# Attention with experts on one core: the row maxima turned by two column-tiled products and sent in one transfer, router logits and experts' sum placed earlier

## The chip, the cores and the metric

One Trainium2 chip, one of its cores. The metric is the device time of one launch in microseconds (us).

## The reference

32 sequences of 256 tokens, 128 wide, pass one pre-norm layer: attention with 16 heads of 8 dimensions, whose softmax is replaced by a rational "stablemax", then a mixture of four experts of which the two with the highest router logits are used.

```python
def stablemax3(logits):                      # over the keys
    logits = logits - max(logits)            # the row maximum
    s = where(x >= 0, 1 + x*(1 + x/2*(1 + x/3)), 1/(1 - x*(1 - x/2*(1 - x/3))))
    return s / sum(s)

x = x + (stablemax3(q @ k.T * hd**-0.5) @ v) @ w_out.T + b_out   # q, k, v of layernorm(x)
xf = layernorm(x)
gates = top-2 of softmax(xf @ router_w + router_b), made to sum to 1
h = silu(einsum('td,edf->etf', xf, w1)) * einsum('td,edf->etf', xf, w3)
x = x + einsum('te,etd->td', gates, einsum('etf,efd->etd', h, w2))
```

## The kernel before, in words

Each sequence ("batch" n, 0 to 31) is one unit of work. A hand-written software pipeline runs over them: `over_batches` calls `first_half` and `second_half` of every engine for n = -2 to 3 written out, for 4 to 27 in a loop of two batches a turn, and for 28 to 31 written out; then `drain`. The engines are TensorE (PE), VectorE (DVE), ScalarE (ACT), GpSimd (POOL) and SyncE (SP, which only issues transfers). Each has its own fixed list of instructions, and semaphores alone join them. From n = 2 on the code takes the branch `settled(n)`.

In the first half of n the core forms the distances of every score from its row's maximum. PE multiplies `q_pad` by `k_stack` (`distances`, L1363), and two rows of `q_pad`, 124 and 125, hold the maxima as a high and a low part, against ones in `k_stack`; so the subtraction is part of the product. ACT squares them (L640), DVE makes a polynomial (L886). Between these PE does the up products of batch n-2's experts: `up_a_unit` and `up_b_unit`, six products each (L1277), whose `a` side goes through silu on ACT (L649) and is multiplied with the `b` side on DVE (`hidden`, L878). POOL weights the hidden units with the gates (L465), which come through DRAM (`gate_scratch`, `gate_all`).

In the second half of n the core forms the scores of batch n+1 (`scores`, L1533), of which DVE keeps only each row's maximum (`scores_max`, L971, eight instructions into `mx`). ACT turns the polynomials of batch n into weights (logarithm L744, exponential L749), PE multiplies them with the values (`weighted_values`, L1295, four groups; products of 32 columns in four column tiles) and forms the experts' down products of batch n-2 (`down`, L1550).

The stretch that the change touches is the end of the second half and the start of the next first half. On PE it is, in this order: weighted values 0 and 1; `maxima_T` (L1594), two transposes that turn `mx` (tokens by heads) into `misc` (16 rows by 256 tokens); `up_a_unit` 0; `queries_and_keys` of batch n+2 (L1277 into `misc`, so it waits for `m_ok`, when the maxima have been read out of it); `router_logits` of batch n-1 (L1584; it waits for `acc_ok`, since the experts' sum lies in the same bank); weighted values 2; `up_b_unit` 0 (waits for `lg_ok`); and then, in the first half, distances 0 and 1 (they wait for the transfers into `q_pad`, `m_stacked`), the values product (L1388, waits for `qk_out`), weighted values 3, the up units 1, distance 2 (waits for polynomial 0).

On DVE it is: the last maximum; `maxima_out`, which adds 1 and splits the maxima into a high part rounded to fp32r (L1020) and the rest (L1022); `experts_added` (L996, signals `acc_ok`); the copy of queries and keys (L985, signals `qk_out`); the logits with their bias (L1003), their maximum and shift (L1010, L1013), four comparisons (L1029, L1030, signal `compared`); four gate steps (L1039, L1042, L1045, L1049), of which the first waits for POOL's `rank` and for ACT's `exp_l` (L793); the input statistics (L858); then hidden 0 and polynomials 0 and 1 of the first half. ACT comes from the last exponential of weights (L749) to `exp_l`, loads a table (L632), does silu 0 and squares 0 and 1. POOL ranks the logits (L567 to L579), adds a bias (L589) and splits queries and keys (L481, L484). SP sends the maxima's two parts, one transfer each (L418, L421), then the output (L426), the gates (L431), and in the first half the queries and keys.

Of the kernel before, what the change touches and what calls it, by code (L numbers as in the profile page):

```python
# [5 lines left out]
def attention_then_experts_kernel(nc: bass.Bass, x: bass.AP, w_qkv: bass.AP, w_out: bass.AP, b_out: bass.AP,  # L6
# [20 lines left out]
    F32 = mybir.dt.float32  # L27
    F32R = mybir.dt.float32r
# [30 lines left out]
    with ctx:  # L59
# [33 lines left out]
        mx = sb("mx", [128, C, H])  # L93
        m_split = sb("m_split", [H, 2, S], F32R)
# [237 lines left out]
        def _(sp):  # L332
# [73 lines left out]
            def second_half(i, off):  # L406
# [8 lines left out]
                if has(i, off + 1):  # L415
                    par = (off + 1) % 2
                    sp.wait_ge(mx_hi_ok, m_split_at)
                    sp.dma_start(q_pad[par][MROW:MROW + 1, :, :, :].bitcast(F32),  # L418
                                 m_split[:, 0, :].bitcast(F32)).then_inc(m_stacked[par], 16)
                    sp.wait_ge(m_ok, m_split_at)  # L420
                    sp.dma_start(q_pad[par][MROW + 1:MROW + 2, :, :, :].bitcast(F32),  # L421
                                 m_split[:, 1, :].bitcast(F32)).then_inc(m_stacked[par], 16)
# [417 lines left out]
        def _(dve):  # L840
# [97 lines left out]
            def second_half(i, off):  # L938
# [29 lines left out]
                def scores_max(u):  # L968
                    dve.wait_ge(s_full, U * (n + 1) + u + 1)
                    by_row = mx[:].rearrange("p c (g j) -> p j c g", j=2)  # L970
# [45 lines left out]
                def maxima_out():  # L1016
                    m = n + 1
                    dve.wait_ge(mT_full, m + 1)
                    after(dve, m_stacked[off % 2], pair_count(i, off, 32))
                    nc.vector.tensor_scalar(m_split[:, 0, :], misc[0:H, 0:S], 1.0, None, ALU.add).then_inc(mx_hi_ok, 1)  # L1020
                    dve.wait_ge(mx_hi_ok, m + 1)
                    nc.vector.scalar_tensor_tensor(m_split[:, 1, :], misc[0:H, 0:S], 1.0, m_split[:, 0, :].bitcast(F32),  # L1022
                                                   ALU.add, ALU.subtract).then_inc(m_ok, 1)
# [29 lines left out]
                if settled(n):  # L1053
# [13 lines left out]
                    if has(i, off + 1):  # L1067
                        scores_max(U - 1)
                        maxima_out()
                    experts_added()  # L1070
                    if has(i, off + 2):
                        queries_and_keys_copied()
                    biased_logits()
                    shifted_logits()
                    compare()
                    for k in range(GATE):
                        gate_step(k)
                    if has(i, off + 3):
                        input_statistics(n + 3)
# [180 lines left out]
        def _(pe):  # L1260
# [86 lines left out]
            def distances(i, off, u):  # L1347

                m, par = no(i, off), off % 2
                if u == 0:  # L1350
                    pe.wait_ge(s_used, U * (m + 1))
                    pe.wait_ge(stacked[par], pair_count(i, off, STACKED))
                    pe.wait_ge(m_stacked[par], pair_count(i, off, 32))
# [13 lines left out]
            def first_half(i, off):  # L1367
# [64 lines left out]
                if settled(n):  # L1432
                    distance(0)
                    distance(1)
                    values()
# [75 lines left out]
            def second_half(i, off):  # L1511
# [75 lines left out]
                def maxima_T():  # L1587
# [5 lines left out]
                    for c in range(C):  # L1593
# [210 lines left out]
```

## Time and profile before

| | us |
|---|---|
| three runs | 1168.31 to 1169.56, median 1169.13 |
| the profiled execution | 1168.15, its span 1166.4 |
| PE busy | 1117.6 (96%) |
| DVE busy | 989.8 (85%) |
| ACT busy | 1002.8 (86%) |
| POOL busy | 746.7 (64%) |

The granted TensorE clock of the profiled execution is 0.995. The span is that of the traced instructions; the execution's own time adds 1.75 us around it. Busy shares are means over the whole span. A batch takes about 34.5 us and its stretches look alike from batch to batch, so one batch in the middle is read instruction by instruction. PEld is PE's loading of weights, which overlaps its products; a product's end in the trace is modelled, so for PE the distances between starts are read.

### The profile page before, as it was taken

How to read it: one execution, taken by the hardware profiler on the slowest of the kernel's cores; microseconds unless marked ns; L12 is line 12 of the kernel's file. 1: busy time of each engine (PE TensorE's matmuls, PEld its weight loads, DVE VectorE, ACT ScalarE, POOL GpSimd, SP SyncE). 2: the span in 40 equal slices, each digit the busy share in tenths (PEclk: the TensorE clock that was granted, in tenths of full speed). 3: DMA queues.
4: the chain of work that ended last, by engine and by line, in shares of the span. 5: the costliest groups of instructions: out<-in, count | busy, mean ns of one | idle time of the engine just before them, and what ended most of it. 6: DMA issues, size and time to landing. Idle time of an engine off the chain costs nothing.

```text
span 1166.4 us, 29175 instructions
## 1 busy us (share of the span) xinstructions
PE 1117.6 (96%) x9904; PEld 942.5 (81%) x9904; DVE 989.8 (85%) x1789; ACT 1002.8 (86%) x1034; POOL 746.7 (64%) x999
## 2 busy tenths in 40 slices
PE   6889999999999999999999999999999999999998
PEld 5758888888888788887888888888887888888888
DVE  4889888899888889888889988888988888988844
ACT  0799899988889998888998888989888899888982
POOL 5347666767666677666676766676766667766530
PEclk8999999999999999999999999999999999999999
DMA  4443333233332233333223333223333222333100
GB/s 127 163 138 115 115 98 92 79 123 115 120 104 89 85 100 117 118 112 94 87 85 118 118 123 100 85 80 113 117 118 107 93 84 94 118 120 108 41 6 11
DMA packets 130063, 117.49 MB, mean 101 GB/s; under 512 B 16452, under 2 KB 124644, under 8 KB 130020
## 3 DMA queue, kind: packets, MB, share of 16 engines
q1 hardware_dynamic: 127812, 113.78, 31.8%
q10 hardware_dynamic: 2208, 3.15, 0.9%
q8 instruction: 26, 0.43, 0.1%
q14 instruction: 17, 0.14, 0.0%
HBM read 94.70 MB, written 21.09 MB: 99 GB/s over the span
## 4 chain that ended last, share of the span: by engine, by line
PE 57%; DVE 14%; issue 12%; POOL 8%; ACT 4%; DMA 2%; DVEq 1%; SPq 0%; ACTq 0%; POOLq 0%
PE banks L1277 23%; PE banks L1550 12%; PE sc L1363 8%; DVE mx L971 5%; DVE poly L886 3%; PE banks L1295 3%; POOL hid L465 3%; PE sc L1533 3%; ACT w_sq L640 1%; PE misc L1277 1%; DMA gate_all<-gate_scratch 1%; ACT poly L744 1%; PE misc L1410 1%; PE misc L1428 1%; PE sc L1277 1%
## 5 line engine op out<-in xcount | busy, mean ns | idle before, releaser
L465 POOL TENSOR_TENSOR hid<-hid,gate_all 128x512 f32<-128x512 f32 x240 | 376.9, 1635 | 155.0 <-DMA gate_all<-gate_scratch 155.0
L886 DVE SCALAR_TENSOR_TENSOR poly<-w_sq,sc 128x1024 f32<-128x1024 f32 x252 | 303.5, 1215 | 23.9 <-ACT w_sq L640 23.6
L1277 PE MATMUL banks<-xn_hi,w_hi 128*128 128x256 f32 x976 | 295.2, 302 | 10.3 <-DVE hid L878 9.7
L640 ACT ACTIVATE w_sq<-sc 128x1024 f32<-128x1024 f32 x252 | 255.3, 1028 | 36.6 <-PE sc L1363 35.6
L1277 PE MATMUL banks<-xn_lo,w_hi 128*128 128x256 f32 x976 | 275.0, 282 | 0.0
L1277 PE MATMUL banks<-xn_hi,w_lo 128*128 128x256 f32 x976 | 274.3, 281 | 0.0
L744 ACT ACTIVATE poly<-poly,two 128x2048 f32<-128x2048 f32 x128 | 252.1, 1992 | 0.4
L1550 PE MATMUL banks<-w_sb,hid 128*128 128x128 f32 x1920 | 247.6, 282 | 0.7 <-POOL hid L465 0.7
L971 DVE TENSOR_REDUCE mx<-sc 128x4 f32<-128x1024 f32 x192 | 230.6, 1216 | 11.0 <-PE sc L1533 9.2
L1550 PEld LDWEIGHTS banks<-w_sb,hid 128*128 128x128 f32 x1920 | 224.1, 191 | 17.7 <-POOL hid L465 1.6
L749 ACT ACTIVATE poly<-poly 128x2048 f32<-128x2048 f32 x128 | 236.7, 1895 | 0.0
L1277 PEld LDWEIGHTS banks<-xn_hi,w_hi 128*128 128x128 f32 x976 | 183.2, 188 | 60.3 <-issue 25.2
L649 ACT ACTIVATE silu_a<-banks 128x512 f32<-128x512 f32 x240 | 144.1, 600 | 59.2 <-PE banks L1277 42.9
L1277 PEld LDWEIGHTS banks<-xn_lo,w_hi 128*128 128x128 f32 x976 | 183.7, 188 | 3.9
L1277 PEld LDWEIGHTS banks<-xn_hi,w_lo 128*128 128x128 f32 x976 | 183.8, 188 | 0.0
L1363 PE MATMUL sc<-q_pad,k_stack 128*128 128x512 f32 x504 | 158.9, 406 | 6.6 <-DVE poly L886 5.3
L878 DVE TENSOR_TENSOR hid<-silu_a,banks 128x512 f32<-128x512 f32 x240 | 160.6, 679 | 0.4
L1295 PE MATMUL banks<-poly,v_pad 128*32 128x256 f32 x2048 | 130.6, 384 | 1.0 <-DVE mx L971 0.7
L1363 PEld LDWEIGHTS sc<-q_pad,k_stack 128*128 128x128 f32 x504 | 78.6, 188 | 18.5 <-DVE poly L886 13.0
L1295 PEld LDWEIGHTS banks<-poly,v_pad 128*32 128x32 f32 x2048 | 56.8, 109 | 40.0 <-issue 7.2
L567 POOL TENSOR_TENSOR equal<-equal,earlier 128x16 f32<-128x16 f32 x62 | 12.3, 220 | 119.7 <-DVE equal L1030 119.7
L971 DVE TENSOR_REDUCE mx<-banks 128x4 f32<-128x1024 f32 x64 | 77.9, 1217 | 0.4 <-PE sc L1533 0.4
(186 smaller groups left out, 1441.4 us busy)
## 6 DMA issues: line engine op xcount, KB each, us to landing
qk_scratch<-qk_split SPq DMA_DIRECT2D x32, 512.0 KB, 3.1
k_tile<-qk_scratch SPq DMA_DIRECT2D x128, 128.0 KB, 2.6
q_pad<-qk_scratch SPq DMA_DIRECT2D x256, 64.0 KB
q_tile<-qk_scratch SPq DMA_DIRECT2D x124, 128.0 KB, 2.5
k_stack<-qk_scratch SPq DMA_DIRECT2D x124, 128.0 KB
gate_all<-gate_scratch SPq DMA_DIRECT2D x30, 512.0 KB, 4.5
x_in<-in_L_attn_x_dram SPq DMA_DIRECT2D x32, 128.0 KB, 2.1
x_res<-in_L_attn_x_dram SPq DMA_DIRECT2D x32, 128.0 KB, 2.3
```

Source lines behind the costliest of these rows:

```text
L465: nc.gpsimd.tensor_tensor(h, h, by_token.unsqueeze(1).to_broadcast([128, 2, C, 128]), ALU.mult).then_inc(gated, 1)
L640: nc.scalar.activation(w_sq[:, u % 2, :], distance_buf(n, u), ACT.Square).then_inc(sq_ok, 1)
L649: nc.scalar.activation(silu_a[:, u % 2, :], up_a[:], ACT.Silu).then_inc(silu_ok, 1)
L744: nc.scalar.activation(poly[:, C * g:C * (g + 1), :], poly[:, C * g:C * (g + 1), :], ACT.Ln, bias=two[:]).then_inc(ln_ok, 1)
L749: nc.scalar.activation(poly[:, C * g:C * (g + 1), :], poly[:, C * g:C * (g + 1), :], ACT.Exp, scale=-1.0).then_inc(p_ok, 1)
L878: nc.vector.tensor_tensor(hid[:, 2 * u:2 * u + 2, :].rearrange("p a t -> p (a t)"), silu_a[:, u % 2, :], b_bank[u], ALU.mult).then_inc(hid ...
L886: nc.vector.scalar_tensor_tensor(poly[:, u, :], w_sq[:, u % 2, :], 3.0, distance_buf(n, u), ALU.add, ALU.mult).then_inc(poly_ok, 1)
L971: nc.vector.tensor_reduce(by_row[:, :, :, u], score_buf[u].rearrange("p (j c t) -> p j c t", j=2, c=C), AX.X, ALU.min, negate=True).then_i ...
L1277: last = nc.tensor.matmul(dst, lhs[a], rhs[b], start=(k == 0), stop=(k == len(terms) - 1))
L1295: last = nc.tensor.matmul(pv[32 * j:32 * j + 32, g // 2, :], v_pad[par][:, c, 4 * g + j, first:first + 32], poly[:, 2 * g + j // 2, at:at ...
L1363: last = nc.tensor.matmul(dst[:, 2 * c * S:2 * (c + 1) * S], k_stack[par][:, u, c * 128:(c + 1) * 128], q_pad[par][:, u, :, :].rearrange(" ...
L1550: last = nc.tensor.matmul(up_b[:, c * D:(c + 1) * D], hid[:, FB * e + f, c * 128:(c + 1) * 128], w2_sb[:, FB * e + f, :], start=(e == 0 an ...
```

## The change

The layout of `mx` becomes heads by column halves, so that one row of it is 32 values, (head, half). `maxima_T` becomes two ordinary float32 products of `mx` (as weights, 32 columns) with the identity, one into rows 0 to 31 and the same again into rows 32 to 63 of `misc`, each 128 wide. `maxima_out` adds 1 and rounds all 64 rows in one instruction, and then overwrites rows 32 to 63 of `m_split` with the rest that rounding left. One transfer takes the 64 rows to both rows of `q_pad`; the waits on `m_stacked` count 16 and no longer 32 per batch. In the settled branch DVE adds the experts' sum ahead of `maxima_out`, takes the logits, their shift and the comparisons ahead of the copy of queries and keys, and the input statistics ahead of the gate steps. PE takes the router products right behind `maxima_T`, and the values product ahead of distances 0 and 1.

```diff
--- before.py
+++ after.py
@@ -90,8 +90,8 @@
         q_pad = [sb(f"q_pad{i}", [128, GP, 2, S], F32R) for i in range(2)]
         ones = sb("ones", [2, S])
         v_pad = [sb(f"v_pad{i}", [128, C, H, 48]) for i in range(2)]
-        mx = sb("mx", [128, C, H])
-        m_split = sb("m_split", [H, 2, S], F32R)
+        mx = sb("mx", [128, H, C])
+        m_split = sb("m_split", [64, 128], F32R)
         w_sq = sb("w_sq", [128, 2, 4 * S])
         poly = sb("poly", [128, U, 4 * S])
         o_T = sb("o_T", [128, G // 2, S])
@@ -414,12 +414,9 @@
                     sp.dma_start(x_in[:], batch_at(x, x_from)).then_inc(x_loaded, 16)
                 if has(i, off + 1):
                     par = (off + 1) % 2
-                    sp.wait_ge(mx_hi_ok, m_split_at)
-                    sp.dma_start(q_pad[par][MROW:MROW + 1, :, :, :].bitcast(F32),
-                                 m_split[:, 0, :].bitcast(F32)).then_inc(m_stacked[par], 16)
                     sp.wait_ge(m_ok, m_split_at)
-                    sp.dma_start(q_pad[par][MROW + 1:MROW + 2, :, :, :].bitcast(F32),
-                                 m_split[:, 1, :].bitcast(F32)).then_inc(m_stacked[par], 16)
+                    sp.dma_start(q_pad[par][MROW:MROW + 2, :, :, :].bitcast(F32),
+                                 m_split[:].bitcast(F32)).then_inc(m_stacked[par], 16)
                 if has(i, off - 2):
                     par = off % 2
                     sp.wait_ge(acc_ok, added)
@@ -967,7 +964,7 @@
 
                 def scores_max(u):
                     dve.wait_ge(s_full, U * (n + 1) + u + 1)
-                    by_row = mx[:].rearrange("p c (g j) -> p j c g", j=2)
+                    by_row = mx[:].rearrange("p (g j) c -> p j c g", j=2)
                     nc.vector.tensor_reduce(by_row[:, :, :, u], score_buf[u].rearrange("p (j c t) -> p j c t", j=2, c=C),
                                             AX.X, ALU.min, negate=True).then_inc(s_used, 1)
 
@@ -1016,11 +1013,11 @@
                 def maxima_out():
                     m = n + 1
                     dve.wait_ge(mT_full, m + 1)
-                    after(dve, m_stacked[off % 2], pair_count(i, off, 32))
-                    nc.vector.tensor_scalar(m_split[:, 0, :], misc[0:H, 0:S], 1.0, None, ALU.add).then_inc(mx_hi_ok, 1)
+                    after(dve, m_stacked[off % 2], pair_count(i, off, 16))
+                    nc.vector.tensor_scalar(m_split[:], misc[0:64, 0:128], 1.0, None, ALU.add).then_inc(mx_hi_ok, 1)
                     dve.wait_ge(mx_hi_ok, m + 1)
-                    nc.vector.scalar_tensor_tensor(m_split[:, 1, :], misc[0:H, 0:S], 1.0, m_split[:, 0, :].bitcast(F32),
-                                                   ALU.add, ALU.subtract).then_inc(m_ok, 1)
+                    nc.vector.scalar_tensor_tensor(m_split[32:64, :], misc[32:64, 0:128], 1.0,
+                                                   m_split[32:64, :].bitcast(F32), ALU.add, ALU.subtract).then_inc(m_ok, 1)
 
                 def compare():
                     for c in range(C):
@@ -1066,17 +1063,18 @@
                         queries_T()
                     if has(i, off + 1):
                         scores_max(U - 1)
+                    experts_added()
+                    if has(i, off + 1):
                         maxima_out()
-                    experts_added()
-                    if has(i, off + 2):
-                        queries_and_keys_copied()
                     biased_logits()
                     shifted_logits()
                     compare()
+                    if has(i, off + 2):
+                        queries_and_keys_copied()
+                    if has(i, off + 3):
+                        input_statistics(n + 3)
                     for k in range(GATE):
                         gate_step(k)
-                    if has(i, off + 3):
-                        input_statistics(n + 3)
                     return
                 statistics()
                 if isinstance(i, int) and n == -2:
@@ -1350,7 +1348,7 @@
                 if u == 0:
                     pe.wait_ge(s_used, U * (m + 1))
                     pe.wait_ge(stacked[par], pair_count(i, off, STACKED))
-                    pe.wait_ge(m_stacked[par], pair_count(i, off, 32))
+                    pe.wait_ge(m_stacked[par], pair_count(i, off, 16))
                     if isinstance(i, int) and 0 <= m < 2:
                         pe.wait_ge(ones_in[par], 16)
                 elif isinstance(i, int) and m < 2:
@@ -1430,9 +1428,9 @@
                     last.then_inc(res_full, 1)
 
                 if settled(n):
+                    values()
                     distance(0)
                     distance(1)
-                    values()
                     weighted_values(i, off - 1, 3)
                     ups(1)
                     distance(2)
@@ -1590,8 +1588,9 @@
                         pe.wait_ge(xn2_out, n)
                     if settled(n) and has(i, off + 2):
                         pe.wait_ge(xnT_ok, n + 3)
-                    for c in range(C):
-                        last = nc.tensor.transpose(misc[0:H, c * 128:(c + 1) * 128], mx[:, c, :], ident[:])
+                    for part in range(2):
+                        last = nc.tensor.matmul(misc[32 * part:32 * (part + 1), 0:128],
+                                                   mx[:].rearrange("p h c -> p (h c)"), ident[:], start=True, stop=True)
                     last.then_inc(mT_full, 1)
 
                 def queries_and_keys():
@@ -1635,10 +1634,10 @@
                     weighted_values(i, off, 1)
                     if has(i, off + 1):
                         maxima_T()
+                    router_logits()
                     up_a_unit(i, off - 1, 0)
                     if has(i, off + 2):
                         queries_and_keys()
-                    router_logits()
                     if isinstance(i, int) and n == B - 1:
                         up_b_unit(i, off - 1, 0)
                         late_up_a(LATE, 1)
```

PE, end of the second half of a settled batch, before (`xn2_hi` and `xn2_lo` are the experts' input, `w1` and `w3` the up weights, `rw` the router's; the last row of each piece opens the first half of the next batch, and rows that repeat are left out):

```order
L1594 MATMUL misc<-ident,mx 16x128 x2
L1277 MATMUL banks<-xn2_hi,w1_hi 128x256
...
L1277 MATMUL misc<-xn_split,proj_hi 128x256 x2
L1277 MATMUL misc<-xn_split,proj_lo 128x256
...
L1584 MATMUL banks<-rw,xn2_T 128x4 x2
L1295 MATMUL banks<-poly,v_pad1 32x256 x8
L1277 MATMUL banks<-xn2_hi,w3_hi 128x256
...
L1363 MATMUL sc<-q_pad0,k_stack0 128x512 x4
L1388 MATMUL misc<-proj_T,xn_T 128x128 x2
```

and now:

```order
L1592 MATMUL misc<-ident,mx 32x128 x2
L1582 MATMUL banks<-rw,xn2_T 128x4 x2
L1275 MATMUL banks<-xn2_hi,w1_hi 128x256
...
L1275 MATMUL misc<-xn_split,proj_hi 128x256 x2
L1275 MATMUL misc<-xn_split,proj_lo 128x256
...
L1293 MATMUL banks<-poly,v_pad1 32x256 x8
L1275 MATMUL banks<-xn2_hi,w3_hi 128x256
...
L1386 MATMUL misc<-proj_T,xn_T 128x128 x2
L1361 MATMUL sc<-q_pad0,k_stack0 128x512 x4
```

The router products have moved ahead of the up unit and of queries and keys, the values product ahead of the distances; the rest stands as it stood.

DVE, from the last maximum of a settled batch to the first hidden product of the next half, before:

```order
L1020 TENSOR_SCALAR m_split<-misc 16x256
L1022 SCALAR_TENSOR_TENSOR m_split<-misc,m_split 16x256
L996 TENSOR_TENSOR y_acc0<-banks,y_acc0 128x256
L985 COPY qk<-misc 128x512
L1003 TENSOR_TENSOR logits<-banks,router_b_all 128x4 x2
L1010 TENSOR_REDUCE top_l<-logits 128x2
L1013 TENSOR_TENSOR shifted<-logits,top_l 128x8
L1029 TENSOR_TENSOR above<-logits 128x16
L1030 TENSOR_TENSOR equal<-logits 128x16
...
L1039 SCALAR_TENSOR_TENSOR chosen<-rank,exp_l 128x8
...
L858 BN_STATS stats<-x_in 128x6 x2
L878 TENSOR_TENSOR hid<-silu_a,banks 128x512
```

and now:

```order
L993 TENSOR_TENSOR y_acc0<-banks,y_acc0 128x256
L1017 TENSOR_SCALAR m_split<-misc 64x128
L1019 SCALAR_TENSOR_TENSOR m_split<-misc,m_split 32x128
L1000 TENSOR_TENSOR logits<-banks,router_b_all 128x4 x2
L1007 TENSOR_REDUCE top_l<-logits 128x2
L1010 TENSOR_TENSOR shifted<-logits,top_l 128x8
L1026 TENSOR_TENSOR above<-logits 128x16
L1027 TENSOR_TENSOR equal<-logits 128x16
...
L982 COPY qk<-misc 128x512
L855 BN_STATS stats<-x_in 128x6 x2
L1036 SCALAR_TENSOR_TENSOR chosen<-rank,exp_l 128x8
...
L875 TENSOR_TENSOR hid<-silu_a,banks 128x512
```

The experts' sum has moved ahead of the split, the copy of queries and keys behind the comparisons, the statistics ahead of the gates.

## Rows read from the trace of the kernel before

**Rows 1.** The page's chain that ended last, by engine.

```profile
PE 57%; DVE 14%; issue 12%; POOL 8%; ACT 4%; DMA 2%; DVEq 1%; SPq 0%; ACTq 0%; POOLq 0%
```

**Rows 2.** Busy time by stretches: stretch, its length, busy time (and instructions) of each engine.

```profile
569.82:579.16 9.34, 8.53 (x81) 6.46 (x77) 6.45 (x21) 8.69 (x10) 4.34 (x10) 1.00 0.07 18
579.16:604.31 25.15, 25.14 (x227) 21.93 (x227) 24.11 (x35) 22.39 (x23) 19.27 (x22) 1.00 0.43 136
```

**Rows 3.** PE in time: start, us, what, records, idle before it and releaser.

```profile
569.82 0.39 PE L1594 MATMUL misc<-ident,mx 128*16 128x128 f32 x2
569.96 0.36 PE L1277 MATMUL banks<-xn_hi,w_hi 128*128 128x256 f32 x1
...
571.20 0.47 PE L1277 MATMUL misc<-xn_split,proj_hi 128*128 128x256 f32 x2 [0.29 <-issue]
...
571.99 0.50 PE L1584 MATMUL banks<-rw,xn_T 128*128 128x4 f32 x4
572.42 1.07 PE L1295 MATMUL banks<-poly,v_pad 128*32 128x256 f32 x16
573.42 0.39 PE L1277 MATMUL banks<-xn_hi,w_hi 128*128 128x256 f32 x1
...
574.24 1.07 PE L1363 MATMUL sc<-q_pad,k_stack 128*128 128x512 f32 x4
...
575.68 1.07 PE L1295 MATMUL banks<-poly,v_pad 128*32 128x256 f32 x16
...
578.03 0.39 PE L1277 MATMUL banks<-xn_hi,w_hi 128*128 128x256 f32 x1 [0.36 <-DVE hid L878]
...
579.16 0.73 PE L1363 MATMUL sc<-q_pad,k_stack 128*128 128x512 f32 x2 [0.15 <-DVE poly L886]
```

**Rows 4.** PE's weight load behind weighted values 2, in time.

```profile
573.42 0.19 PEld L1277 LDWEIGHTS banks<-xn_hi,w_hi 128*128 128x128 f32 x1 [0.41 <-issue]
```

**Rows 5.** DVE in time.

```profile
568.40 1.22 DVE L971 TENSOR_REDUCE mx<-sc 128x4 f32<-128x1024 f32 x1
570.24 0.41 DVE L1020 TENSOR_SCALAR m_split<-misc 16x256 fp32r<-16x256 f32 x1 [0.62 <-PE misc L1594]
570.69 0.41 DVE L1022 SCALAR_TENSOR_TENSOR m_split<-misc,m_split 16x256 fp32r<-16x256 f32 x1
571.03 0.40 DVE L996 TENSOR_TENSOR y_acc<-banks,y_acc 128x256 f32<-128x256 f32 x1
572.19 0.69 DVE L985 COPY qk<-misc 128x512 f32<-128x512 f32 x1 [0.76 <-PE misc L1277]
572.80 0.22 DVE L1003 TENSOR_TENSOR logits<-banks,router_b_all 128x4 f32<-128x4 f32 x2
...
575.17 0.41 DVE L1039 SCALAR_TENSOR_TENSOR chosen<-rank,exp_l 128x8 f32<-128x8 f32 x1 [1.41 <-POOL rank L579]
...
576.10 0.89 DVE L1049 TENSOR_TENSOR gates<-chosen,chosen_r 128x8 f32<-128x8 f32 x1
...
577.89 2.34 DVE L886 SCALAR_TENSOR_TENSOR poly<-w_sq,sc 128x1024 f32<-128x1024 f32 x2
```

**Rows 6.** ACT in time.

```profile
569.64 3.70 ACT L749 ACTIVATE poly<-poly 128x2048 f32<-128x2048 f32 x2
573.45 0.21 ACT L793 ACTIVATE exp_l<-shifted 128x8 f32<-128x8 f32 x1
...
575.61 1.94 ACT L640 ACTIVATE w_sq<-sc 128x1024 f32<-128x1024 f32 x2
```

**Rows 7.** POOL in time: its first split of queries and keys.

```profile
575.93 1.03 POOL L481 TENSOR_TENSOR qk_split<-qk,zero 128x512 fp32r<-128x512 f32 x1
```

**Rows 8.** Transfers by line: issues, KB each, median us from issue to landing.

```profile
q_pad<-m_split SPq DMA_DIRECT2D x64, 16.0 KB, 2.2
gate_scratch<-gates SPq DMA_DIRECT2D x30, 4.0 KB, 1.4
```

**Rows 9.** The page's DMA queues: packets, MB, share of 16 engines' span.

```profile
q1 hardware_dynamic: 127812, 113.78, 31.8%
```

## The prediction

> **What bounds the kernel now.** I read the page's chain first: PE carries 57% of the chain that ended last, DVE 14%, and 12% is "issue" [rows 1]. The kernel is a pipeline of nearly equal periods. I cut one of them in two with the view of busy time by stretches [rows 2]; its parts are 9.34 and 25.15 us long. From the maxima's turn (569.82) to the third distance product of the next batch (579.16) PE is busy 8.53 us; from there to the next turn (604.31) it is busy 25.14 us. The second piece is PE's alone and the change hardly touches it. Everything that can be won lies in the first 9.34 us, and every edit lies there.
>
> What PE waits for in this stretch is read from its starts in order of time [rows 3]. I price each block by the distance to the next start where nothing is waited for:
> - the turn, 569.82 to 569.96: 0.14
> - a unit of six up products, 573.42 to 574.24: 0.82; there are four of them in the stretch: 3.28
> - queries and keys, 571.20 to 571.99: 0.79
> - router products, 571.99 to 572.42: 0.43
> - a group of weighted values, 572.42 to 573.42: 1.00; two: 2.00
> - distances 0 and 1 with the values product, 574.24 to 575.68: 1.44
>
> Together 8.08 us. (The other group of weighted values, at 575.68, and the other up units have the same form.) The stretch takes 9.34, so PE stands still for 1.26 us in it: before the queries and keys (they wait for the maxima's split on DVE, m_ok, which ends at 571.10), before the second up_b unit (578.03; it waits for DVE's first hidden product) and before distance 2 (it waits for DVE's first polynomial, 577.89 and 1.22 long, so done at 579.11; PE goes on at 579.16) [rows 3, 5].
>
> Why is DVE late there? Before that polynomial it waits 0.62 for the turned maxima, 0.76 for the queries and keys and 1.41 for POOL's rank [rows 5]. The rank needs DVE's comparisons, the last of which ends at 573.76 (575.17 less 1.41), and these are late because the logits come last on PE and behind the copy of queries and keys on DVE.
>
> **The change, part by part.** I place everything on the clock of the period shown, with the last maximum ending at 569.62.
>
> Experts' sum ahead of the split: the 0.40 us of the sum [rows 5] now run from about 569.54 to 569.94, inside DVE's 0.62 us wait. Cost nothing; if the turn came at once instead, it would cost the split 0.3.
>
> The turn: two transposes of 16 columns become two float32 products of 32 columns, in two column groups. A float32 product is two records on this PE (four for the two router products at 571.99) [rows 3], so four records in place of two. Then the router follows at once, and it needs the experts' sum (acc_ok, at about 570.0). Its start is not in the trace. Lower bound: the sum's end and PE's reaction, 570.06, which is 0.10 later than the 569.96 at which PE now goes on. Upper bound: after a group of column-tiled products the full-width weight load stood still for 0.41 us [rows 4]; 0.41 on top of the old slot. I take 0.24, since the products are short (128 columns against 256 in the row with 0.41) and run in two groups at once. So PE's work is 8.08 + 0.24 = 8.32 us, between 8.18 and 8.49.
>
> The same weight-load gap bears on a rule: the Trainium skill, TensorEngine Tiling (Array Packing), section Tiling Modes, says that changing the tiling mode drains the engine, and under Restrictions that column tiling excludes the transpose mode for float32. By that rule the full-mode transposes now pay a drain after the weighted values, and tiled products would not pay it: only the drain behind them would remain, the change would add about nothing to PE, and the time would come out 28.5 x 0.24, some 7 us, under the sum below. The trace cannot tell this, since before the old turn the weight load waits 0.41 us for DVE's maximum as well.
>
> The split: each of its two DVE instructions walks 128 elements and not 256. The 128x512 copy takes 0.69 and the 16x256 instruction 0.41 [rows 5], so 256 elements are 0.28 and 128 are 0.14: 0.27 each. They end near 570.95 and not 571.10. PE reaches the queries and keys at 570.20 + 0.43 + 0.82 = 571.45, later than that: the first wait is gone, 0.45 us.
>
> Logits earlier: router products end near 570.75, DVE takes the logits at 570.95 right behind the split. From the logits to the last comparison's end there were 0.96 us (572.80 to 573.76), so now 571.9, where it was 573.76. POOL's rank between them and chosen took 1.41 us (573.76 to 575.17) [rows 5], so chosen could start at 573.3.
>
> What is late next is ACT: its last exponential of weights ends at 573.34 and exp_l came at 573.45 [rows 6]; it can come at 573.27, since the engines begin an instruction some 0.08 before the recorded end of the last one. Gain only 0.18 there. So chosen at about 573.55 and the gates done by 575.4, where they were 576.99 [rows 5]. Square 0 then starts 2.16 after exp_l, as it did (573.45 to 575.61, table load and silu 0 between them) [rows 6], at 575.43, ending 0.97 on (two take 1.94); polynomial 0 runs from 576.5 to 577.7. By ACT and DVE distance 2 could start at 577.75.
>
> Copy of queries and keys behind the comparisons: PE starts them at 571.45, the copy came 0.99 after their start (571.20 to 572.19) [rows 3, 5], so 572.45 to 573.15; DVE is free from 571.9, nothing is lost. Waiting for it: POOL's split of them (at 575.93 before [rows 7]) and now PE's values product. Input statistics ahead of the gates: 0.4 us of DVE, in the time that it would wait for exp_l.
>
> Values ahead of distance 0 on PE: PE comes there at 571.45 + 0.79 + 1.00 + 0.82 = 574.1, 0.9 us after the copy. No wait. Distance 0 moves to about 574.6, still before ACT needs it (575.43).
>
> One transfer for two on SP: issue at about 571.1, landing 2.2 us after [rows 8], 573.3; distance 0 wants it at 574.6. One issue less on SP, which has no one behind it.
>
> **Sum.** PE reaches distance 2 after 8.32 us, at 578.14; ACT and DVE would allow 7.93. PE decides. Gain per batch 9.34 - 8.32 = 1.02 us, with 0.85 and 1.16 at the bounds. From then on PE is the chain, and ACT and DVE follow it. The reordered part runs in 29 batches (2 to 30; the last has no queries and keys and gets half), so 28.5 x 1.02 = 29 us, and under 1 us in the filling. Against the profiled execution's 1168.15 that is 1139; the median of the runs shown is 1169.13, 1 us more, so I say **1139**.
>
> **Rivals.**
> (a) The turn costs PE nothing more: a gap ahead of the old transposes, hidden in the wait for the maximum, goes, and only one behind the products comes. Then PE's 8.08 decide, 9.34 - 8.08 = 1.26 per batch, 1132; ACT's 7.93 would allow 1.41 and 1128 at most. For it: the gap comes after every group of column-tiled products, wherever that stands. Against: the router still needs the experts' sum. Chance 0.10. This is the way the rule of the Trainium skill named above would have it.
> (b) DVE stays late. The gates instruction took 0.89 us for eight elements at 576.10 [rows 5], while POOL's split ran until 576.96 [rows 7]; POOL's split of queries and keys can now start earlier and hold it, twice if it falls badly, for about 1.3 us more. Then the gates are done at 576.6 and not 575.4, the polynomial starts 0.6 later as it did (hidden 0 lies between), lasts 1.22, and distance 2 comes at about 578.5 to 578.9: gain 0.4 to 0.8, 1145 to 1157, in the middle 1151. Chance 0.13.
> (c) The gain is given back in the second piece (by the gates' transfer, or by ACT), or PE's idle time only moves: within 0.2% of before, which is about what a measurement of this kernel can tell from no change. Against: 25.14 of 25.15 us there are PE's own work. Chance 0.05.
> (d) Slower, by the transfer. Two transfers of 16 pieces become one of 64 pieces into two partitions. Packets took 0.318 x 16 x 1166 / 127812 = 46 ns of one DMA engine each [rows 9]. If all 64 go through one engine, that is 3.0 us on top of 2.2: landing at 576.3, and distance 0 waits 1.7 us for it. It costs more than it gains once the landing takes 4.5 us: +0.7 per batch, 1188. Against: the gates' store, also of many small rows, lands in 1.4 us [rows 8]. Chance 0.07.
>
> **How the numbers follow.** The forecast has 0.65, (a) 0.10, (b) 0.13, (c) 0.05, (d) 0.07. Faster by over 0.2%: 0.88; within: 0.05; slower: 0.07. The forecast's own range is 1135 to 1144 from the bounds of the turn (28.5 x 1.16 and 28.5 x 0.85), and 2 us more on each side for starts read to a few hundredths; with most of (a) and (b) the range is 1130 to 1155, and (c), (d) stay outside.
>
> **What would show it.** In the changed profile: the period falls to about 33.5 us; PE's wait before the queries and keys is gone, and so are those for the first hidden product and for polynomial 0; the last comparison ends some 2.1 us after the turn's start and not 3.94; chosen waits for ACT's exp_l and not for POOL; the transfer lands in 2.1 to 2.5 us. It is wrong if distance 0 waits for a DMA, if the values product waits for DVE, or if the router's first record starts over 0.6 us after the turn.

## The result, and the profile after

The changed kernel takes 1129.05 us, median of 4 runs (1128.44 to 1130.74), against 1168.84 us before, median of 4 (1168.31 to 1169.56). The ratio is 0.966, 95% interval 0.9645 to 0.9678: 3.4% faster, about 40 us. The forecast was 1139 in a range from 1130 to 1155; the sign is right, the gain is a third larger than forecast, and the time lies 1 us below the range. The profiled execution took 1130.74 us with a span of 1129.0, so against the one of before (1168.15, span 1166.4) there are 37.4 us to explain.

The page's chain of the changed kernel, by engine, to be held against [rows 1]:

```profile
PE 90%; ACT 4%; DVE 3%; DMA 1%; issue 1%; ACTq 0%; SPq 0%; DVEq 0%
```

PE has gone from 57% to 90% of the chain. Busy time by stretches in the same columns as [rows 2], cut at the same places, the turn at 553.18 and the third distance product at 561.42:

```profile
553.18:561.42 8.24, 8.24 (x82) 6.25 (x79) 6.27 (x21) 8.21 (x11) 4.48 (x10) 1.00 0.16 51
561.42:586.42 25.00, 24.99 (x229) 21.91 (x227) 23.90 (x36) 22.98 (x25) 19.23 (x22) 1.00 0.41 126
```

The first piece has shrunk from 9.34 to 8.24 us and PE is busy in all of it. The second went from 25.15 to 25.00. The granted clock is 1.00 in both columns before and after, so none of this is the clock.

PE in time, which answers to [rows 3]:

```profile
553.18 0.39 PE L1592 MATMUL misc<-ident,mx 128*32 128x128 f32 x4
553.58 0.58 PE L1582 MATMUL banks<-rw,xn_T 128*128 128x4 f32 x4
554.01 0.37 PE L1275 MATMUL banks<-xn_hi,w_hi 128*128 128x256 f32 x1
...
554.81 0.40 PE L1275 MATMUL misc<-xn_split,proj_hi 128*128 128x256 f32 x2
...
555.61 1.07 PE L1293 MATMUL banks<-poly,v_pad 128*32 128x256 f32 x16
556.61 0.38 PE L1275 MATMUL banks<-xn_hi,w_hi 128*128 128x256 f32 x1
...
557.42 0.61 PE L1386 MATMUL misc<-proj_T,xn_T 128*128 128x128 f32 x4
557.79 1.17 PE L1361 MATMUL sc<-q_pad,k_stack 128*128 128x512 f32 x4
...
558.89 1.07 PE L1293 MATMUL banks<-poly,v_pad 128*32 128x256 f32 x16
559.89 0.39 PE L1275 MATMUL banks<-xn_hi,w_hi 128*128 128x256 f32 x1
...
561.42 0.62 PE L1361 MATMUL sc<-q_pad,k_stack 128*128 128x512 f32 x2
```

No row of PE's products carries a wait any more. The turn takes 0.40 us until the router products start (four records for two products, as read), and the queries and keys follow the up unit after 0.80 us without a gap. Two of PE's weight loads do stand still:

```profile
553.15 0.15 PEld L1592 LDWEIGHTS misc<-ident,mx 128*32 128x32 f32 x4 [0.27 <-DVE mx L968]
553.54 0.52 PEld L1582 LDWEIGHTS banks<-rw,xn_T 128*128 128x128 f32 x4 [0.24 <-issue]
```

The second is put down to no one, but it begins 0.12 us after the recorded end of the experts' sum (553.01 and 0.41 long, below), which the router products wait for by the program. The section on the order alone comes back to it.

DVE in time, which answers to [rows 5]:

```profile
551.88 1.22 DVE L968 TENSOR_REDUCE mx<-sc 128x4 f32<-128x1024 f32 x1
553.01 0.41 DVE L993 TENSOR_TENSOR y_acc<-banks,y_acc 128x256 f32<-128x256 f32 x1
553.62 0.28 DVE L1017 TENSOR_SCALAR m_split<-misc 64x128 fp32r<-64x128 f32 x1 [0.19 <-PE misc L1592]
553.94 0.28 DVE L1019 SCALAR_TENSOR_TENSOR m_split<-misc,m_split 32x128 fp32r<-32x128 f32 x1
554.25 0.23 DVE L1000 TENSOR_TENSOR logits<-banks,router_b_all 128x4 f32<-128x4 f32 x2
...
555.06 0.17 DVE L1027 TENSOR_TENSOR equal<-logits 128x16 f32<-128x16 f32 x1
555.72 0.69 DVE L982 COPY qk<-misc 128x512 f32<-128x512 f32 x1 [0.49 <-PE misc L1275]
556.33 0.47 DVE L855 BATCH_NORM_STATS2 stats<-x_in 128x6 f32<-128x128 f32 x2
557.02 0.45 DVE L1036 SCALAR_TENSOR_TENSOR chosen<-rank,exp_l 128x8 f32<-128x8 f32 x1 [0.22 <-ACT exp_l L790]
...
557.99 0.48 DVE L1046 TENSOR_TENSOR gates<-chosen,chosen_r 128x8 f32<-128x8 f32 x1
558.92 0.69 DVE L875 TENSOR_TENSOR hid<-silu_a,banks 128x512 f32<-128x512 f32 x1 [0.45 <-ACT silu_a L646]
559.89 2.35 DVE L883 SCALAR_TENSOR_TENSOR poly<-w_sq,sc 128x1024 f32<-128x1024 f32 x2 [0.29 <-ACT w_sq L637]
```

The reader is to see three things. The sum at 553.01 lies beside the turn, and of DVE's wait for the turned maxima 0.19 us are left, where there were 0.62. The last comparison ends at 555.23, 2.05 us after the turn's start (forecast 2.1, before 3.94). Chosen, hidden 0 and polynomial 0 now all wait for ACT: polynomial 0 is done at 561.11 and PE comes to distance 2 only at 561.42, so DVE is 0.3 us early and PE decides.

To see what one batch in the middle does not show, I took the starts of every PE block in the 27 periods from the first settled turn on, and their means, before and after (us from block start to the next block's start; worked out from the two traces):

```
                                         before   changed
turn, to the next block                   0.141     0.407
router products                           0.432     0.438
up_a 0 (before: with the wait for m_ok)   1.288     0.799
queries and keys                          0.786     0.801
weighted values 2                         1.001     1.000
up_b 0                                    0.817     0.815
distances 0, 1 and values                 1.443     1.463
weighted values 3                         1.001     1.001
up units 1 (before: with the wait)        2.472     1.533
= first piece                             9.38      8.26
distance 2                                0.569     0.463
two up units behind distance 3            1.521     1.443
second down block                         2.933     2.883
weighted values 0, 1, to the turn         1.867     1.774
= second piece, all blocks               25.21     24.96
period                                   34.59     33.22
```

A batch has gained 1.12 us in the first piece and 0.25 us in the second: 1.37 us, and 28 of them are 38 us. (The span shrank by 37.4: in this execution the first settled turn came 0.9 us later than before, 121.28 and not 120.41, and the end was 0.3 us shorter.)

### The profile page after: what moved, and what is told of

It is laid out like the page before. It is cut to its first block, busy times and chain, and to the rows that moved or that the text cites. A ratio compares the mean times of both kernels' runs of the same rounds, so it can differ in the third digit from the quotient of the medians.

```text
span 1129.0 us, 29283 instructions
## 1 busy us (share of the span) xinstructions
PE 1104.0 (98%) x9968; PEld 936.7 (83%) x9968; DVE 980.8 (87%) x1789; ACT 1004.1 (89%) x1034; POOL 750.7 (66%) x999
## 4 chain that ended last, share of the span: by engine, by line
PE 90%; ACT 4%; DVE 3%; DMA 1%; issue 1%; ACTq 0%; SPq 0%; DVEq 0%
PE banks L1275 33%; PE banks L1548 20%; PE sc L1361 11%; PE banks L1293 10%; PE sc L1531 4%; PE misc L1275 2%; ACT poly L741 2%; PE banks L1582 2%; ACT poly L746 1%; PE misc L1408 1%; PE misc L1426 1%; PE misc L1386 1%; PE banks L1531 1%; PE sc L1275 1%; DVE mx L968 1%
## 5 line engine op out<-in xcount | busy, mean ns | idle before, releaser
L1275 PE MATMUL banks<-xn_hi,w_hi 128*128 128x256 f32 x976 | 289.3, 296 | 0.2
L1361 PE MATMUL sc<-q_pad,k_stack 128*128 128x512 f32 x504 | 161.3, 411 | 2.6 <-DVE poly L883 1.6
L1531 PE MATMUL sc<-k_tile,q_tile 32*128 32x256 f32 x768 | 65.8, 333 | 7.3 <-DMA q_tile<-qk_scratch 4.4
```

Of the source, the lines that this page charges most:

```text
L1275: last = nc.tensor.matmul(dst, lhs[a], rhs[b], start=(k == 0), stop=(k == len(terms) - 1))
L1361: last = nc.tensor.matmul(dst[:, 2 * c * S:2 * (c + 1) * S], k_stack[par][:, u, c * 128:(c + 1) * 128], q_pad[par][:, u, :, :].rearrange(" ...
```

## The experiments

Each has a time as median, and the mean period with its first piece, cut as above. "Before" was timed again beside them, in three groups: 1170.1, 1169.5 and (for the last of them, the gates' route) 1169.9 us.

### Which part carries it: the order alone

```diff
 the changed kernel's order on PE and DVE, with, from the kernel before:
+ mx [128, C, H]; m_split [H, 2, S]; two transposes; split of 16x256 twice
+ two transfers; m_stacked counts 32
```

> The new order on every engine, but the old turn (two transposes into 16 rows) and two transfers. Theory (the order frees PE's three waits, the new turn matters little): 1129 to 1133 us. The stretch from the turn to distance 2 keeps its 8.3 us, because the router still starts only when the experts' sum is done, about 0.3 to 0.4 after the turn; only the start of the turn after weighted values 0 comes some 0.09 later than in the changed kernel (1.86 and not 1.77 us after them). Rival (the turn and its shorter split carry a large part): above 1140 us, with PE waiting before queries and keys.

1131.02 us (ratio to before 0.966, 0.9642 to 0.9674). The period is 33.22 us, first piece 8.17 and second 25.05: the theory holds and the rival is out. In the settled batches the new turn is worth nothing once the order is new. The two forms differ on either side of the turn: weighted values 0 and 1 take 1.87 us until the turn with transposes and 1.77 with products; the turn takes 0.32 us until the router with transposes and 0.41 with products. From weighted values 0 to the router it is 2.18 us either way.

That the two add up to the same is not a property of the turn. In both kernels the experts' sum on DVE releases the router. In the order-only kernel:

```profile
552.77 0.41 DVE L996 TENSOR_TENSOR y_acc<-banks,y_acc 128x256 f32<-128x256 f32 x1
553.06 0.39 PE L1595 MATMUL misc<-ident,mx 128*16 128x128 f32 x2
553.30 0.52 PEld L1585 LDWEIGHTS banks<-rw,xn_T 128*128 128x128 f32 x4
553.34 0.58 PE L1585 MATMUL banks<-rw,xn_T 128*128 128x4 f32 x4
```

The sum ends at 553.18 and the router's weights are loaded from 553.30. In all 27 periods of each of the eight kernels that have the router right behind the turn, that load begins 0.115 to 0.117 us after the sum's recorded end, however far the turn lies from it (0.13 us before that end in some batches, 1.62 in others). The sum itself stands behind DVE's last maximum, which ends 1.66 to 1.74 us after the start of weighted values 0 in nearly all batches of both kernels.

### The turn alone

```diff
 the kernel before, with, from the changed one:
+ mx [128, H, C]; m_split [64, 128]; two products of 32 columns; split in place
+ one transfer; m_stacked counts 16
```

> The old order, with the products, the 64-row split and the single transfer. Theory: the split ends about 0.2 us sooner and everything behind it on DVE follows, PE's waits for hidden 0 and polynomial 0 stay: gain 0.15 to 0.3 us per batch, 1160 to 1165 us. Rival (the turn carries the gain): below 1150 us.

1160.47 us (ratio 0.991, 0.9894 to 0.9927); the period is 34.36 us, 0.23 less than before. As expected: in the old order a shorter split moves DVE's whole chain forward; but it is a small part of the gain (a sixth by the periods; 9.6 of 39 us, a quarter, by the medians), and the order alone already has all of it. This kernel has an up unit behind the turn, which does not wait for the sum, and so shows the turn's own cost: 0.32 us until the up unit, against 0.14 behind the transposes.

### DVE: the copy of queries and keys ahead of the logits

```diff
                     if has(i, off + 1):
                         maxima_out()
+                    if has(i, off + 2):
+                        queries_and_keys_copied()
                     biased_logits()
                     shifted_logits()
                     compare()
-                    if has(i, off + 2):
-                        queries_and_keys_copied()
```

> The changed kernel, with DVE's copy of queries and keys ahead of the logits again. Theory: the last comparison ends 1.5 to 2 us later, chosen waits for POOL's rank again, polynomial 0 ends about 0.5 us after PE wants it: 1140 to 1145 us, with PE waiting before distance 2. Rival (early logits on PE alone are enough, DVE has slack): 1129 to 1131 us.

1171.42 us (ratio 1.0008, 0.9998 to 1.0018): this one place on DVE takes back all of the gain. I was right that it costs and far off in how much: 42 us more than the changed kernel, where I had expected 11 to 16. The period is 34.72 us with a first piece of 9.25 (1.0 more) and a second one 0.51 longer. ACT in time, and DVE's end of the stretch, of this kernel (its turn is at about 570.5):

```profile
574.40 0.21 ACT L790 ACTIVATE exp_l<-shifted 128x8 f32<-128x8 f32 x1 [0.78 <-DVE shifted L1010]
```

```profile
576.12 0.41 DVE L1036 SCALAR_TENSOR_TENSOR chosen<-rank,exp_l 128x8 f32<-128x8 f32 x1 [1.02 <-POOL rank L576]
576.56 0.16 DVE L1039 TENSOR_REDUCE chosen_sum<-chosen 128x2 f32<-128x8 f32 x1
576.76 0.17 DVE L1042 RECIPROCAL chosen_r<-chosen_sum 128x2 f32<-128x2 f32 x1
577.05 0.89 DVE L1046 TENSOR_TENSOR gates<-chosen,chosen_r 128x8 f32<-128x8 f32 x1
577.86 0.68 DVE L875 TENSOR_TENSOR hid<-silu_a,banks 128x512 f32<-128x512 f32 x1
```

I had left out that the late shift holds ACT's exp_l (0.78 us) and that the gates meet POOL's split again (0.89 us for eight elements and not 0.48). The longer second piece I had not foreseen at all; it is taken up below.

### DVE: the experts' sum behind the split

```diff
-                    experts_added()
                     if has(i, off + 1):
                         maxima_out()
+                    experts_added()
                     biased_logits()
```

> The changed kernel, with the experts' sum behind the split again. Theory: the router right behind the turn waits for the sum, about 1.1 us on PE per batch, so 28 x 1.1 on top of 1129: 1155 to 1162 us, all of it an idle PE between turn and router. Rival (PE has slack for it elsewhere): under 1140 us.

1172.19 us (ratio 1.0017, 1.0007 to 1.0026), 10 us above my upper figure. PE of this kernel in time:

```profile
571.87 0.39 PE L1592 MATMUL misc<-ident,mx 128*32 128x128 f32 x4
573.51 0.58 PE L1582 MATMUL banks<-rw,xn_T 128*128 128x4 f32 x4 [1.25 <-DVE y_acc L993]
```

From turn to router there are 1.64 us where there were 0.40. The sum starts at 572.94 behind the split and ends at 573.36. It is an idle PE as the theory says, priced 0.2 short; the mean period grew by 1.52 us, 1.29 of it here and the rest in the three blocks behind. Early router products on PE are thus worth something only together with the early sum on DVE.

### PE: the router products behind queries and keys

```diff
                         maxima_T()
-                    router_logits()
                     up_a_unit(i, off - 1, 0)
                     if has(i, off + 2):
                         queries_and_keys()
+                    router_logits()
```

> The changed kernel, with PE's router products behind queries and keys again (DVE's order as changed). Theory: DVE takes the logits 1.6 us later and the copy of queries and keys behind them about 1.1 us later; PE waits a little before the values product and polynomial 0 ends at about the moment that PE wants it: 0.1 to 0.4 us per batch, 1132 to 1140 us. Rival (the early router products carry most of the gain): above 1150 us.

1150.95 us (ratio 0.984, 0.9822 to 0.9852): outside my figures and at the rival's. The first piece is 8.51 us, 0.26 more, in the middle of what I expected, and that alone would have been about 1136. The rest is in the second piece, which is 0.55 longer: the second down block takes 3.34 us and not 2.88. PE there:

```profile
586.48 1.16 PE L1548 MATMUL banks<-w_sb,hid 128*128 128x128 f32 x8
587.89 2.05 PE L1548 MATMUL banks<-w_sb,hid 128*128 128x128 f32 x16 [0.25 <-POOL hid L462]
```

PE waits in the down products for POOL's weighting of hidden units with the gates. So the logits' place acts twice: some 5 us later on hidden 0 and polynomial 0, and over 20 us later on the down products, by way of gates, DRAM, `gate_all` and POOL's eight weightings of 1.6 us.

### The gates' route by itself

```diff
 on SP, the store of the gates moved from the second half
 to behind the store of queries and keys in the next first half:
+                    sp.wait_ge(gates_ok, gates_made)
+                    after(sp, gates_in, gates_read)
+                    sp.dma_start(gate_scratch, gates[off % 2]...).then_inc(gates_out, 16)
                     sp.wait_ge(gates_out, gates_at)
```

> The changed kernel, with SP sending the gates to DRAM behind the store of queries and keys, and nothing else moved: the gates reach POOL about 1.7 us later. Theory (the gates' route, DRAM, gate_all and POOL's eight weightings, had 0.2 us of slack before the change, has about 0.7 in the changed kernel, and took 0.44 us per batch from the kernels with the late logits): the first piece of the period stays at 8.26 us, the second down block stretches by about 1.0 us, 28 x 1.0: 1150 to 1160 us. Rival (the longer down block in those kernels had another cause): 1129 to 1133 us.

1165.82 us (ratio 0.9965, 0.9952 to 0.9977), above my upper figure and far from the rival's. The first piece is 8.24 us against 8.26, and the second down block takes 4.22 us, 1.34 more. SP's loads of keys behind `gate_all` are issued only 0.2 us later (10.08 us after the turn and not 9.87), and no other block of PE grew by over 0.01 us. PE there:

```profile
594.74 1.16 PE L1546 MATMUL banks<-w_sb,hid 128*128 128x128 f32 x8
596.89 2.05 PE L1546 MATMUL banks<-w_sb,hid 128*128 128x128 f32 x16 [0.99 <-POOL hid L460]
```

POOL's weightings start 13.85 us after the turn's start (turn at 570.56) and not 11.82 (565.00 less 553.18), 2.03 us later; PE lost 1.34. So the route has about 0.7 us of slack in the changed kernel, which is what I had read off, and the miss is in how late a store in the second place comes (2.0 and not 1.7). Before the change the same reading gives 0.2: POOL's last weighting of the batch shown ended at 595.91, and PE wanted it at about 596.16 (its second down block began at 595.18, and the first eight of its 24 records, which need less, take a third of 2.93). In some batches it was not enough (the block's longest was 3.42 us against 2.87).

### PE: the values product behind distances 0 and 1

```diff
-                    values()
                     distance(0)
                     distance(1)
+                    values()
                     weighted_values(i, off - 1, 3)
```

> The changed kernel, with the values product behind distances 0 and 1 again. Theory: the maxima's transfer has landed before distance 0 even 0.36 us earlier, and the values product waits for nothing: 1128.5 to 1130 us, no change. Rival (the single transfer of 64 rows lands late and the values product covers it): distance 0 waits for a DMA, above 1132 us.

1129.80 us (ratio 0.966, 0.9647 to 0.9673): no change. Distance 0 starts 0.36 us earlier and the maxima have landed even so.

### DVE: the input statistics behind the gates

```diff
-                    if has(i, off + 3):
-                        input_statistics(n + 3)
                     for k in range(GATE):
                         gate_step(k)
+                    if has(i, off + 3):
+                        input_statistics(n + 3)
```

> The changed kernel, with DVE's input statistics behind the gates again. Theory: the gates are done before silu 0 either way, so hidden 0 starts when it did: 1128.5 to 1130 us, no change. Rival (hidden 0 comes 0.4 us later and PE feels it): 1133 us or more.

1129.60 us (ratio 0.966, 0.9645 to 0.9672), period 33.21: no change.

### A version meant to be better: weighted values 2 beside 3

```diff
                     values()
                     distance(0)
                     distance(1)
+                    if not (isinstance(i, int) and n == 2):
+                        weighted_values(i, off - 1, 2)
                     weighted_values(i, off - 1, 3)
 ...
-                    weighted_values(i, off, 2)
+                    if isinstance(i, int) and n == B - 1:
+                        weighted_values(i, off, 2)
```

> The changed kernel, with weighted values 2 moved from the second half to directly ahead of weighted values 3. Theory (a fixed loss of 0.13 to 0.2 us follows each return from column-tiled to full-width products, and PE is the bound): one return less per batch, 28 x 0.13 to 0.2 us, 1123 to 1126 us. Rival (other waits take it up, for instance the values product for DVE's copy, which it now reaches 1.0 us sooner): 1128 us or more, with a wait before the values product or distance 0.

1140.10 us (ratio 0.975, 0.9735 to 0.9761): the rival's way. The pair takes 1.87 us where the two groups took 2.00, so the 0.13 us are there. But PE now comes 1.0 us sooner to the values product and to distance 0, and waits at both in the batch shown:

```profile
559.93 0.52 PEld L1386 LDWEIGHTS misc<-proj_T,xn_T 128*128 128x128 f32 x4 [0.28 <-DVE qk L982]
560.64 0.76 PEld L1361 LDWEIGHTS sc<-q_pad,k_stack 128*128 128x128 f32 x4 [0.19 <-DMA q_pad<-m_split]
```

The first piece is 8.64 us, 0.38 more. The second row also times the single transfer: issued at 557.71, it lets PE go on at 560.64, 2.93 us later. I had counted 2.2 from the start of the issue. In the changed kernel the issue is at 554.25, so the data are usable at about 557.18, and distance 0 comes at 557.79: 0.6 us of slack, not 1.3.

## Why the prediction came out as it did

**The bound, and the wait before queries and keys: right.** PE carries the chain, all three waits in the first piece are gone, and the split's end no longer matters there. One wait is new: the router's, for the experts' sum. (The wait before queries and keys was 0.42 us by the prediction's own price of an up unit, 1.24 less 0.82, and not 0.45; no sum used it.)

**The turn: the size right by luck, 0.24 us forecast and 0.27 measured** (0.407 less 0.141). The forecast took the 0.24 from the idle weight load behind column-tiled products. What sets the router's start is the path that it had named only as its lower bound, the experts' sum and PE's reaction: that path gave 0.24 us after the turn's start with the turn where it was (0.28 at the shortest in the order-only kernel), and 0.39 to 0.42 here, because the turn starts about 0.1 us sooner after weighted values 0 and the sum does not. From weighted values 0 to whatever follows the turn it was 2.01 us before and is 2.18 now, with either form: the router's place behind the sum costs 0.17, and the form of the turn nothing on top.

The turn's own cost shows where an up unit follows. In the router-back kernel the turn comes 1.75 us after weighted values 0 and the up unit 0.32 later, together 2.07; before the change it was 1.87 and 0.14, together 2.01. The rule of the Trainium skill, TensorEngine Tiling (Array Packing), section Tiling Modes, that changing the mode drains the engine, agrees with these traces: the transposes stand 0.11 us later behind the tiled weighted values than the products do, and the full-width work behind the products is held longer. The rule's other consequence that I drew, that the products add nothing, holds to 0.06 us. Whether PE would reach the router 0.09 us sooner (0.32 and not 0.41, an estimate from these rows; 2.5 us in 28 batches) if DVE took the sum ahead of its last maximum was not run.

**The logits: right in order and time.** The comparisons end 2.05 us after the turn (2.1 forecast); chosen waits for ACT and no longer for POOL; distance 2 could start 7.98 us after the turn (561.16), where 7.93 was forecast. The copy-first and router-back kernels show that it is this place that pays: one step back on DVE costs 42 us, one on PE 22.

**The blocks of the first piece: mis-sized by 0.11 us.** The step "a unit of six up products: 0.82; there are four of them: 3.28" counts the weight load behind a change of work in each unit. It shows only in the first of a row: two units without a wait take 1.53 us, not 1.64. The forecast was 8.32 us for the piece, and 8.26 came; against a mean of 9.38 before (I took the 9.34 of one batch, and the batches alternate between 9.33 and 9.44) that is 1.12 and not 1.02.

**"The second piece is PE's alone and the change hardly touches it": this is the step that failed.** It gave 0.25 us per batch as cut, 7 us in all; a term for it would have put the forecast at 1132. Of the 0.25, 0.09 are the turn's: it starts sooner behind weighted values 0, and with the sum setting the router's start this comes back in the first piece. The 0.16 that are left (4.5 us) are the second piece's own, and the order-only kernel has just these (25.21 to 25.05). PE's 25.14 busy of 25.15 us hid small losses, since a product's recorded duration includes what it waits for its weights: 0.11 at distance 2 and 0.08 in the two up units behind distance 3 (both came straight after a wait for DVE, with weights not yet loaded: 0.569 and 1.521 us before, 0.463 and 1.443 after), and 0.05 in the down block, where the gates came late. Two other blocks grew by 0.09 together. The kernels with a late polynomial 0 bear the first two out: the copy-first and router-back kernels, whose PE waits for it, have 0.57 and 1.52 us in these blocks again, and the sum-back kernel, whose PE does not, has 0.46 and 1.44.

**The rivals.** (a), 1132 with 1128 as the end, was nearest to the time, though for a sum of small terms and not for its one. (b), gates held by POOL: the gates step took 0.48 us in the batch shown and 0.90 in about every second one, and ended 0.02 to 0.03 us after POOL's split in each (in the batch shown 557.40 and 1.04 long), but hidden 0 waits for ACT's silu in any case (0.45 and 0.28 us). The Trainium skill, GPSIMD Engine Reference, section Specifications, says that POOL shares its SBUF interfaces with VectorE, with contention for DVE instructions that have two SBUF inputs; the gates instruction is one, and this case agrees: 0.17 us at the shortest, 0.48 to 0.98 where POOL's split was running. (c), gain given back: the gates' route, which I named there, got slack from the change, from 0.2 to 0.7 us; it would have taken gain back if the logits had stayed late. (d), the transfer: 64 pieces are usable 2.93 us after the issue begins, so they do not go one behind the other through one engine at 46 ns in addition to the 2.2.

**The range** ended at 1130 because I counted the blocks' uncertainty at 2 us in all. 28 batches multiply a tenth of a microsecond to 3: the second piece had no term of its own, and with the up units (0.11) and the net of the turn (0.17 and not 0.24) that is most of the 0.35 us per batch, 10 us in all, that the forecast's 1.02 lacked.

## What to carry to other kernels

An engine that is busy in 99.9% of a stretch may still be waiting in it: compare the same block's start-to-start time where it follows a wait and where it does not, and count the difference as something that a change can free. When an order is changed in a steady pipeline, follow each moved result to all its readers, also to the ones 20 us away; the logits paid a third (copy first) to two thirds (router back) of their price there. When two forms of a step cost the same, look first at whether either of them is what the next step waits for. A step of 8 elements that many engines wait for belongs ahead of a 512-element copy that nobody needs yet, and to move one step of a chain without the others (router without sum, router without logits) gained nothing here.

## What the runs showed of the hardware that was not expected

- Between column-tiled work and a full-width up unit, a turn by two float32 transposes of 16 columns took 2.01 us from weighted values 0 (1.87 and 0.14, before), one by two column-tiled products of 32 columns 2.07 (1.75 and 0.32, router-back kernel).
- The weight load of the router products began 0.115 to 0.117 us after the recorded end of DVE's sum that releases them, in 216 batches of eight kernels, though the profile names no releaser for its idle time (0.24 us, "issue").
- One change less from full-width to column-tiled products and back saves 0.13 us: two groups together take 1.87 us, apart 2.00.
- An up unit of six products takes 0.72 us behind another one or behind a distance product and 0.80 to 0.82 behind weighted values, the router products or a transpose, with PE recorded as busy throughout.
- A DVE instruction of eight elements with two SBUF inputs took 0.17 us alone and up to 0.98 while a POOL instruction on 128x512 ran.
- The transfer of 64 rows of 512 bytes into two partitions released its waiter 2.93 us after its issue began.
